# Four attention layers on one core: first values taken from the input loop's page, padding moved ahead of that loop, and the check of a top-32 flag count moved behind the next mask

## The reference

```python
# first sublayer, 16 heads of 16
q, k, v = (query @ Wq + bq), (key_value @ Wk + bk), (key_value @ Wv + bv)
attn = jax.nn.softmax(clip(einsum('bhqd,bhkd->bhqk', q, k) * scale, -CLAMP, CLAMP), axis=-1)
x = x + einsum('bhqk,bhkd->bqhd', attn, v).reshape(B, Nq, Cq) @ Wo + bo
# third sublayer, 4 heads of 32
scores = einsum('bthd,bghd->bhtg', Q, K) / sqrt(32)
topv, topi = jax.lax.top_k(scores, 32)
probs = jax.nn.softmax(topv, axis=-1)
attn = jnp.zeros_like(scores).at[bi, hi, ti, topi].set(probs)
attn_mean = attn.mean(axis=1)      # over the 4 heads
c_t = einsum('btg,bgd->btd', attn_mean, V)
```

## Time and profile before

| | |
|---|---|
| median of 3 runs | 2983.53 us (2981.58 to 2985.75) |
| the profiled execution | 2974.51 us, of which its span 2972.7 us |
| TensorE (PE) busy | 2295.7 us, 77% of the span |
| VectorE (DVE) / ScalarE (ACT) / GpSimd (POOL) busy | 1460.9 / 1457.4 / 916.9 us |
| chain that ended last, by engine | PE 44%, DVE 17%, POOL 13%, issue 12%, ACT 7%, DMA 3% |
| mean granted TensorE clock | 0.879 of full speed |

### The profile page before, as it was taken

One profiled execution on the slowest core, in us unless ns is written; L12 is line 12 of the kernel. 1 busy time (PEld: TensorE's weight loads), 2 busy tenths in 40 slices (PEclk: granted clock), 3 DMA queues, 4 the chain that ended last, 5 costly groups with the idle time before them and its releaser, 6 DMA issues.

```text
span 2972.7 us, 36678 instructions
## 1 busy us (share of the span) xinstructions
PE 2295.7 (77%) x12668; PEld 1301.9 (44%) x12668; DVE 1460.9 (49%) x4388; ACT 1457.4 (49%) x2266; POOL 916.9 (31%) x471
## 2 busy tenths in 40 slices
PE   0566599999973998568888658897667898668897
PEld 0522222323222665346555346555346555346555
DVE  8656001121222121686553686553696553696553
ACT  3143387787760222571365571365571365571365
POOL 1023100101102111471094471094372094270094
PEclk9988799999986999668998769998769998769999
DMA  2045834443252111103022103022103022103023
GB/s 61 0 159 175 156 46 82 59 77 53 45 171 70 45 46 42 40 1 117 1 48 44 42 1 117 1 48 43 43 1 117 0 48 44 35 1 110 0 26 47
DMA packets 176789, 168.16 MB, mean 57 GB/s; under 512 B 84064, under 2 KB 147168, under 8 KB 176576
## 3 DMA queue, kind: packets, MB, share of 16 engines
q1 hardware_dynamic: 169088, 156.36, 22.4%
q0 software_dynamic: 7504, 9.35, 1.7%
HBM read 133.52 MB, written 32.32 MB: 56 GB/s over the span
## 4 chain that ended last, share of the span: by engine, by line
PE 44%; DVE 17%; POOL 13%; issue 12%; ACT 7%; DMA 3%; SPq 1%; another core or an unknown queue 1%; DVEq 1%; POOLq 0%; ACTq 0%; PEldq 0%
PE ps L1287 5%; POOL sb_arena L724 5%; PE ps L1298 4%; POOL sb_xtn L722 4%; ACT sb_arena L947 3%; DVE sb_xnT L2305 2%; PE ps L1457 2%; PE ps L1677 2%; PE ps L1625 2%; PE ps L1476 2%; PE ps L1470 2%; PE ps L1695 2%; PE ps L1605 2%; PE ps L1614 2%; PE ps L1596 2%
## 5 line engine op out<-in xcount | busy, mean ns | idle before, releaser
L947 ACT ACTIVATE sb_arena<-ps 128x1024 f32<-128x1024 f32 x416 | 402.7, 1021 | 136.3 <-PE ps L1287 132.5
L2305 DVE MAX8 sb_xnT<-sb_arena 128x8 f32<-128x60 f32 (+1 forms) x1728 | 246.9, 206 | 70.8 <-ACT sb_arena L1042 70.8
L1287 PE MATMUL ps<-sb_arena 96*128 96x512 bf16 x832 | 234.5, 387 | 29.0 <-ACT sb_arena L947 13.7
L2464 DVE TENSOR_REDUCE sb_arena<-ps 128x2 f32<-128x1024 f32 x128 | 156.3, 1223 | 202.4 <-PE ps L1695 201.9
L836 POOL TENSOR_TENSOR sb_arena<-sb_arena 128x1601 f32<-128x1601 f32 x56 | 176.5, 3151 | 217.8 <-DVE sb_arena L2293 217.6
L1524 PE MATMUL ps<-sb_arena,sb_xnT 32*128 32x400 f32 (+1 forms) x512 | 162.0, 719 | 85.4 <-ACT sb_arena L1042 81.8
L1298 PE MATMUL ps<-sb_arena 128*32 128x512 f32 x1664 | 224.5, 612 | 1.5 <-ACT sb_arena L947 1.5
L724 POOL TENSOR_TENSOR sb_arena<-sb_arena,sb_xtn 128x1024 f32<-128x1024 f32 (+1 forms) x112 | 206.8, 1846 | 8.8
L771 POOL DMA_INDIRECT taken_rows<-sb_taken,sb_slots x32 | 31.3, 980 | 565.3 <-DVEq L2072 556.8
L1125 ACT ACTIVATE sb_arena<-ps 128x512 f32<-128x512 f32 x256 | 151.9, 593 | 88.9 <-PE ps L1663 88.5
L722 POOL TENSOR_TENSOR sb_arena<-sb_arena 128x1024 f32<-128x1024 f32 (+1 forms) x16 | 24.4, 1526 | 539.3 <-DVEq L2421 534.3
(11 more groups left out here) (348 smaller groups left out, 4499.8 us busy)
## 6 DMA issues: line engine op xcount, KB each, us to landing
sb_arena<-in_ctxT SPq DMA_DIRECT2D x13, 1601.0 KB, 7.4
sb_arena<-k_spill SPq DMA_DIRECT2D x96, 208.0 KB, 8.5
sb_arena<-in_dft SPq DMA_DIRECT2D x5, 2048.0 KB, 7.8
k_spill<-sb_arena SPq DMA_DIRECT2D x12, 832.0 KB, 5.2
sb_arena<-in_w SPq DMA_DIRECT2D x16, 512.0 KB, 6.4
sb_arena<-in_idft SPq DMA_DIRECT2D x4, 2048.0 KB, 8.6
sb_arena<-in_wf SPq DMA_DIRECT2D x8, 1024.0 KB, 11.9
o_rows<-sb_arena SPq DMA_DIRECT2D x32, 256.0 KB, 2.3
```

The costliest lines, as they stand in the source:

```text
L947: A(probs0[:, 2 * (m % 4):2 * (m % 4) + 2, :], ps[:, 2 * (m % 2):2 * (m % 2) + 2, :], ACT.Exp).then_inc(pair_probs, 1)
L1287: ins = mm(ps[:, 2 * (m % 2) + i, :], k_stack[0:NSPLIT, h, k * P:(k + 1) * P], q_stack[0:NSPLIT, h, :], start=True, stop=True)
L2305: ins = V.max(cand[:, n % 2, 8 * j:8 * j + 8], s_sb[:, n % 6, c0:c0 + w])
```

## The change

Part one, around the input loop. The fifth page now holds batch 0's context, so that the loop leaves it in `ctxT`; the load of batch 0 into `ctx0` is gone, and `ctx0` serves from batch 1 on (one wait count less). The padding of `v0_b`, and that of `v0_a` from chunk 6 on, moves ahead of the input loop on GpSimd; chunks 0 to 5 of `v0_a`, whose words the loop uses, are padded after `close_input`. TensorE makes chunks 0 to 4 of the first values before `close_input`, chunks 5 to 12 behind it, on seven banks with no wait for VectorE. VectorE takes them up inside each branch of the flag, ahead of the attention. TensorE waits for all padding inside the branch.

Part two, in the top-32 stage. For odd n, `settle` and `weight` of head n-1 move from step k = 6 to behind the mask pass of head n. For odd n ScalarE copies the count before `scale_head(n-1)` rather than behind it.

```diff
+        V0_AT = o
         v0_a = at(o, [KCH, H0 * V0W]); o += KCH * H0 * V0W
...
+        EARLY_PADS = 6
+        EARLY_VALUES = 5
...
-            sp.dma_start(ctx0[:, :, :], a["ctxT"][0].rearrange("(c p) k -> p c k", p=P)).then_inc(ctx0_loaded, 16)
             for g in range(4):
                 stacks(0, g)
...
             pool.sem_inc(in_squares, 1)
+
+            def pads(i, k0, k1):
+                vpad = v0s[i].rearrange("p k (h w) -> p k h w", w=V0W)
+                G.memset(vpad[:, k0:k1, :, D0 + 1:V0W], 0.0).then_inc(v0_pads, 1)
+                G.memset(vpad[:, k0:k1, :, D0:D0 + 1], 1.0).then_inc(v0_pads, 1)
+
+            def last_pads(i, n):
+                vpad = v0s[i].rearrange("p k (h w) -> p k h w", w=V0W)
+                pool.wait_ge(v0_pads, n - 1)
+                G.memset(v0s[i][P // 2:P, KCH - 1, :], 0.0).then_inc(v0_pads, 1)
+                pool.wait_ge(v0_pads, n)
+                G.memset(vpad[0:KW[-1], KCH - 1, :, D0 + 1:V0W], 0.0).then_inc(v0_pads, 1)
+                G.memset(vpad[0:KW[-1], KCH - 1, :, D0:D0 + 1], 1.0).then_inc(v0_pads, 1)
+
+            pads(1, 0, KCH - 1)
+            last_pads(1, 3)
+            pads(0, EARLY_PADS, KCH - 1)
+            last_pads(0, 8)
             with pool.Fori(0, NBATCH) as b:
...
-            for i, v in enumerate(v0s):
...
             pool.wait_ge(table_cleared, 16)
             close_input(pool)
+            pads(0, 0, EARLY_PADS)
+            pool.wait_ge(v0_pads, 12)
...
-                    if 1 <= n < TILES * H1 - 1:
+                    if n % 2 == 0 and n >= 1:
                         scale_head(n - 1)
                     act.wait_ge(count_done, nth(b, count_done, n + 1))
                     A(kept[0:1, n:n + 1], ps[0:1, 7, 3 * P:3 * P + 1], ACT.Copy, scale=1.0 if n % 2 else -1.0).then_inc(count_ready, 1)
+                    if n % 2 and n < TILES * H1 - 1:
+                        scale_head(n - 1)
...
+            def first_values(k0, k1):
+
+                for k in range(k0, k1):
+                    for c in range(CTXCH):
+                        ins = mm(ps[0:KW[k], k // 2, k % 2 * DIM:(k % 2 + 1) * DIM], ctxT[:, c, k * P:k * P + KW[k]], wv0[:, c, :],
+                                 start=(c == 0), stop=(c == CTXCH - 1))
+                    if k0:
+                        ins.then_inc(v0_done, k0 + 1 if k == k0 else 1)
+
+            pe.wait_ge(in_ctx, 16 * NBATCH + 16)
+            first_values(0, EARLY_VALUES)
             close_input(pe)
-            for k in range(KCH):
-                values(0, k, k % 4, 0, 4)
+            first_values(EARLY_VALUES, KCH)
             with pe.If(use_general != 0):
+                pe.wait_ge(v0_pads, 12)
...
             with pe.Else():
+                pe.wait_ge(v0_pads, 12)
...
-            dve.wait_ge(v0_pads, 10)
             dve.wait_ge(x_loaded, 16 * NBATCH)
             close_input(dve)
-            for k in range(KCH):
-                values_in(0, k, k % 4, 0, k + 1)
...
             with dve.Else():
                 steps[0], n_ln[0], n_ln[1] = mark
+                for k in range(KCH):
+                    values_in(0, k, k // 2, k % 2 * DIM, min(KCH, k // 2 * 2 + 2))
...
-                        if k == (4 if (n - 1) % 2 else 6) and n >= 1:
+                        if k == 4 and n >= 1 and n % 2 == 0:
                             settle(n - 1)
                             weight(n - 1)
                         search(n + 1, k)
...
                         V.tensor_scalar(kept01[:, 1, 0:GKEYS], s, least, 0.0, ALU.is_ge, ALU.add, accum_out=kept_by_row[:, 1, :]).then_inc(choice_ready, 1)
+                        settle(n - 1)
+                        weight(n - 1)
...
-        "ctxT": np.stack([rows(c.T) for c in g["ctx_768"]] + [np.zeros((CTXCH * P, GKEYS), f)]),
+        "ctxT": np.stack([rows(c.T) for c in g["ctx_768"]] + [rows(g["ctx_768"][0].T)]),
```

More of the change, by code:

```diff
@@ L225, in program @@
         head_sum_w = at(o, [DCH, QUARTER]); o += DCH * QUARTER
-        assert o <= CTX0_AT
+        assert o <= V0_AT + EARLY_PADS * H0 * V0W
         o = 0
@@ L753, in _ @@
             pool.wait_ge(in_spilled_k, 48 * NBATCH + 1)
-            for i, v in enumerate(v0s):
-                vpad = v.rearrange("p k (h w) -> p k h w", w=V0W)
-                G.memset(v[P // 2:P, KCH - 1, :], 0.0).then_inc(v0_pads, 1)
-                pool.wait_ge(v0_pads, 5 * i + 1)
-                G.memset(vpad[:, 0:KCH - 1, :, D0 + 1:V0W], 0.0).then_inc(v0_pads, 1)
-                G.memset(vpad[:, 0:KCH - 1, :, D0:D0 + 1], 1.0).then_inc(v0_pads, 1)
-                pool.wait_ge(v0_pads, 5 * i + 3)
-                G.memset(vpad[0:KW[-1], KCH - 1, :, D0 + 1:V0W], 0.0).then_inc(v0_pads, 1)
-                G.memset(vpad[0:KW[-1], KCH - 1, :, D0:D0 + 1], 1.0).then_inc(v0_pads, 1)
-                pool.wait_ge(v0_pads, 5 * i + 5)
             pool.wait_ge(table_cleared, 16)
             close_input(pool)
+            pads(0, 0, EARLY_PADS)
+            pool.wait_ge(v0_pads, 12)
             for b in range(NBATCH):
@@ L1210, in values @@
                 if k == 0:
-                    pe.wait_ge(ctx0_loaded, nth(b, ctx0_loaded, 16))
+                    pe.wait_ge(ctx0_loaded, nth(b - 1, ctx0_loaded, 16))
                     if b >= 2:
```

## The result

Over four runs each, the changed kernel takes 2930.66 us (2928.43 to 2937.11), the kernel before 2982.74 (2981.58 to 2985.75): a ratio of 0.983, 95% interval 0.9814 to 0.9846, so 52.1 us less, where 53.6 were forecast. The same kernel, twice more on other occasions, gave 0.9836 (0.9823 to 0.9849) and 0.9826 (0.9813 to 0.984): 49 and 51 us.

What follows compares the result with a forecast made beforehand. No engine bounds throughout; VectorE is nearest to the bound in the top-32 stage. Part one 18.2 plus part two 35.4 make 53.6 us off 2974.5, 2920.9; with 9.0 to the median, forecast 2930, range 2917 to 2951 (8 in 10).

Steps and rivals of the forecast that it cites:

- Early values: Input loop: TensorE's 20 matmuls for chunks 0 to 4 take 6.4 us, end at 305.7; engines meet at about 305.9.
- Stack: Before first attention: without the ctx0 load, the first quad's stack is complete 13.1 us after first issue, at about 319.2.
- Branch: Before first attention: TensorE's branch, 9.6 us from last matmul to first score, ready at 322.7; other bound 2.5 us.
- Memsets: First normalisation: moved memsets, about 6.1 us on GpSimd, hold up VectorE by 0.3 us; bounds zero and 4.7.
- Waits of the even heads: Top-32 stage: 28 waits of VectorE before even heads' reciprocals, 1.09 us each, go behind the mask: 30.5 us.
- the register load: Top-32 rival: load doesn't run beside the mask, 0.8 and 0.18 us reappear, only 6.4 remain: 2959; chance 0.05.
- Give-back: Top-32 stage: the even heads' loop has 0.05 to 0.4 us slack before the scores; 1.5 us lost over all.
- End of a stage: At n = 15 the mask fills the 3.0 us wait; each stage ends 1.6 us early, 6.4 in all.
- The scores: Top-32 rival: scores become the bound, every pair loses 0.5 us, part two gives 21: 2944; chance 0.14.
- VectorE's branch: Before first attention, rival: VectorE's branch costs 15 us, its additions end at 327, part one gives 14: 2934; chance 0.1.
- GpSimd's queue: Top-32 rival: queue falls behind, VectorE waits some 2.9 us per pair, 26 slower than before: 3009; chance 0.03.

Runs made afterwards that it cites:

- experiment 3: Kernel before with only batch 0's ctx0 load gone: ratio 0.997; kernel before with only the memsets moved early: 0.9986.
- experiment 4: Changed kernel with head 9's flag checked at candidate step 6 of head 10 instead of step 4: ratio 0.9844, changed kernel 0.9836.
- experiment 5: Changed kernel without the count's copy ahead of the scaling: 1.003, 2990.5 us; kernel before with only that edit: 0.9992.

## Why the prediction was right, and where it wasn't

**Sum.** 2930 forecast, 2930.7 measured. The parts hit less well: the start gave 17.6 to 19.5 us in the three traces of the changed kernel (18.2 forecast), the stages 32.4 to 33.3 (35.4). The lower end of the range was added up wrong: 22, 36.9 and 4 us off 2983.5 are 2920.6, not 2917. That the profiled execution lay 9 us under the median was taken over, and that was right: other profiles of kernels with the old start or the old stage are longer in stretches that the change doesn't touch (tail and experts 312.1 us in before, 313.5 to 316.4 in all thirteen others).

**Early values.** Predicted from 299 to 305.7 in 6.4 us; measured 298.8 to 306.3, 7.5 us. In this execution and the third (7.6 us) some sixteen and nineteen of the twenty matmuls ran at a granted clock of 0.50; in the second it rose at 303 us, after eleven, as I had supposed, and the values took 6.3. Meeting at 306.6 instead of 305.9.

**Stack.** Predicted complete 13.1 us after its first issue; it took 16.0 (15.6 and 15.7 in the other two executions, 15.5 with the load gone alone). Taking 6 us off the 19.1 for the load that stood ahead was the step that failed; it was worth 3.1 to 3.6.

**Branch.** The 9.6 us from last matmul to first score was the wrong quantity, as experiment 3 shows; in the changed kernel it would have been 5.0, and with the stack late by 3.4 us the two errors cancelled. The number 322.7 was right for a wrong reason, and so by luck.

**Memsets.** They ran from 153.6 to 160.2 us. VectorE's four scalings beside one of them:
```profile
157.38 1.29 POOL L750 MEMSET sb_arena<- 128x1440 f32 x1
157.77 2.39 DVE L1904 TENSOR_SCALAR sb_xtn<-sb_xtn,sb_ln_mv,sb_ln_rstd 128x256 f32<-128x256 f32 x4
```
In the kernel before, they took 1.38 (0.41 for the first). Here the first took 1.05 and ended just behind the memset, so it was held for some 0.65 us, and the four for 1.0 us in all; TensorE's first projection began at 162.87, beside 162.78 before; as the pass began 0.26 us earlier, some 0.35 is left behind the cover. I took 0.3, bounds 0 to 4.7. The rule of the Trainium skill (SBUF — State Buffer, "Who interferes with whom") had given 1 us, and for the hold itself the trace agrees; of the 0 to 1 us that it left behind the cover, the trace shows about a third.

**Waits of the even heads.** 30.5 us were to go, and went: no pause behind 28 masks, so the register load and the branch fit beside the mask, as the earlier trace rows had shown for another operation. That rival is out.

**Give-back.** 1.5 us, sought in the scores. VectorE waited for the scores only where a stage begins (ahead of its first two heads' searches); the loop that I had put at 0.05 to 0.4 us of slack held. The give-back was in the odd heads' flags: without those at n = 15 the waits before odd reciprocals rose from 8.7 to about 14 us, nearly all of the rise at head 9. I had followed ScalarE, GpSimd and VectorE round the loop, and TensorE's queue only as far as the counts of one pair, not as far as head 8, where a context product and scores both stand ahead of the next count.

**End of a stage.** The wait at n = 15 fell from 12.4 us in sum to 4.7; the mask fills 1.9 of each 3.0. From the copy of head 14's count to the last count it is 2.1 us in batch 1 where it was 3.4, so 1.3 early (1.6 forecast, from the earlier trace rows), as TensorE there waits for the copies of transposed probabilities and no longer for the mask. Behind it VectorE lost 1.6 us per stage in a way that I hadn't seen. The second execution of after, and the same instruction 5.7 us on:
```profile
1759.63 3.02 POOL L839 TENSOR_TENSOR sb_arena<-sb_arena 128x1601 f32<-128x1601 f32 x1 [2.17 <-ACT sb_arena L1073]
...
1760.92 3.41 DVE L2381 SCALAR_TENSOR_TENSOR sb_arena<-sb_arena 128x1601 f32<-128x1601 bf16 x1
...
1766.62 1.83 DVE L2381 SCALAR_TENSOR_TENSOR sb_arena<-sb_arena 128x1601 f32<-128x1601 bf16 x1
```
VectorE's product with two inputs takes 3.41 us beside GpSimd's and 1.83 alone. In the old order it came just behind GpSimd's. It showed in the stage ends, 69.0 to 71.4 us in the kernels with the old stage and 73.7 to 78.0 in those of after. Where TensorE's last product but one ran at the higher clock throughout (6.07 us), it then idled 1.58 us for VectorE in the old order (one stage of the kernel before) and 2.70 in the new, and the last product behind it took 6.07 us in the old and 7.96 to 8.07 in the new. So the delay seems to show once as itself and once more through the clock (0.50 in the window of experiment 4). Over the whole it can't be told from scatter: from last count to the end of the batch both kinds take the same, 1148 to 1154 us and 1151 to 1155.

**The rivals.** The scores, the register load and VectorE's branch (additions from 310.1, 3.6 us behind the meeting, done at 314.5) didn't come. Nor did GpSimd's queue. The nearest to a slower kernel was half the change (experiment 5).

## What to carry to other kernels

Where a pause is removed by moving a step, two engines' orders usually have to change together: here one edit alone was 25 us slower in its stage, the other worth 4, both 32.6. Follow every queue of the loop over a full period, not over one pair, for the next wait stands at the one place where the period has an extra operation. And before a stretch behind a branch is priced, look for the branch's own record, and compare more than one profile of a kernel: two executions differed by as much as a small change is worth.

## What the runs showed of the hardware

The record of TensorE's branch was 3.6 to 3.9 us where it began together with the first of the stacks' transfers and 8.6 to 13.0 us with the DMA engines full (share 1.05 to 1.08). The longer ones start 3 to 4 us before the engine's last matmuls end; counted from there the branch ended after 3.9 to 4.2 us where it came first, 4.6 to 5.6 with early values, and 9.0 to 10.1 in the old place. The rule of the Trainium skill (Runtime: NRT & Kernel Launch, "Instruction fetch mechanics"), that a taken branch out of the window fetches its target by DMA, fits: in every trace a 16-KB packet of instructions is served inside that record, 2.6 to 3.6 us ahead of its end.

VectorE was held by GpSimd according to the form of its instruction: the scalings, 256 columns in float32 each, for some 0.65 us beside a memset, the product with two inputs for 1.6 us beside a product, while the mask pass, which also sums its row, took 1.88 us beside GpSimd's 3.02 as it does alone.

The clock level made one and the same work on TensorE cost 3.17 or 5.92 us, and through the order of its queue this reached VectorE. At the stage's end the same product took 6.07 us where TensorE had idled 0.56 to 1.58 us ahead of the transposes, and 7.96 to 8.72 us where it had idled 2.70; what experiment 4 had gained on VectorE was lost there.
